# A fused transformer layer in fp16 pairs: the order of VectorE's and TensorE's work in slots 1 to 3, the first loads, and the norm scales

## What is computed

```python
ln_out = layernorm(hidden_states, ln1_s, ln1_b)
qkv = ln_out @ w_qkv + b_qkv
q, k, v = jnp.split(qkv, 3, axis=-1)
ctx = merge_heads(attention(split_heads(q), split_heads(k), split_heads(v), ltor_mask))
x = hidden_states + ctx @ w_ao + b_ao
ln_out = layernorm(x, ln2_s, ln2_b)
q = ln_out @ w_q + b_q
k, v = jnp.split(encoder_states @ w_kv + b_kv, 2, axis=-1)
ctx = merge_heads(attention(split_heads(q), split_heads(k), split_heads(v), cross_mask))
x = x + ctx @ w_co + b_co
ln_out = layernorm(x, ln3_s, ln3_b)
return x + gelu(ln_out @ w1 + b1) @ w2 + b2

def attention(q, k, v, mask):
    scores = jnp.einsum('bhqd,bhkd->bhqk', q, k) / jnp.sqrt(jnp.float32(HD))
    scores = scores * mask - 10000.0 * (1.0 - mask)
    return jnp.einsum('bhqk,bhkd->bhqd', jax.nn.softmax(scores, axis=-1), v)
```

## Time and profile before

| | |
|---|---|
| median of 3 runs | 1778.62 us (1777.15 to 1781.05) |
| the profiled execution | 1779.09 us |
| its span, first to last instruction | 1777.3 us |
| mean granted TensorE clock, as a share of full speed | 0.995 |
| busy in the span: TensorE, its weight loads | 1689.2, 1032.7 us |
| VectorE, ScalarE, GpSimd | 1033.2, 1036.9, 658.8 us |

### The profile page before, as it was taken

The page is one execution under the profiler, slowest core; times in us unless marked ns, Lnnn a source line. Parts: engine busy times, 40 slices in busy tenths (PEclk is TensorE's granted clock), DMA queues, the critical chain, the costliest instruction groups (busy, mean ns, idle before and its releaser), DMA issues. The chain is left out here.

```text
span 1777.3 us, 40192 instructions
## 1 busy us (share of the span) xinstructions
PE 1689.2 (95%) x13342; PEld 1032.7 (58%) x13342; DVE 1033.2 (58%) x3584; ACT 1036.9 (58%) x3138; POOL 658.8 (37%) x812
## 2 busy tenths in 40 slices
PE   3899999999999999999999997999999999999999
PEld 2567676766766766767667663444444444444444
DVE  6877777777776677777777764623233332324221
ACT  3677777778877777777788865532323232323332
POOL 0456556565654554655555642202020201010110
PEclk9999999999999999999999999999999999999999
DMA  5332223222231232332222312310101020202010
GB/s 157 98 103 92 89 86 100 86 64 88 92 102 52 82 111 92 112 100 97 91 94 99 116 40 94 96 60 13 59 12 65 6 66 5 71 0 71 0 48 24
DMA packets 83236, 130.31 MB, mean 73 GB/s; under 512 B 14144, under 2 KB 22336, under 8 KB 83136
## 3 DMA queue, kind: packets, MB, share of 16 engines
q1 hardware_dynamic: 83136, 129.04, 22.6%
HBM read 103.83 MB, written 25.17 MB: 73 GB/s over the span
## 5 line engine op out<-in xcount | busy, mean ns | idle before, releaser
L1253 POOL TENSOR_TENSOR a_p_s<-a_p_s,a_rcp 128x512 f32<-128x512 f32 x256 | 266.6, 1041 | 444.5 <-DVE a_rcp L889 444.4
L758 ACT ACTIVATE a_p_s<-a_t_s,a_mx 128x128 f32<-128x128 f32 x1024 | 398.7, 396 | 10.0 <-DVE a_mx L880 10.0
L1437 PE MATMUL m_ps_y<-w,m_g_r 128*128 128x512 f16 x1536 | 353.2, 379 | 0.0
L1423 PE MATMUL m_ps_h<-mlp_xT,w 128*128 128x512 f16 x1536 | 349.8, 379 | 2.0 <-PEq L407 1.7
L1522 DVE SCALAR_TENSOR_TENSOR m_g_r<-m_g_t,up_by,m_g_r 128x512 f16<-128x512 f32 x128 | 103.3, 807 | 407.0 <-ACT m_g_r L1495 406.6
L1423 PEld LDWEIGHTS m_ps_h<-mlp_xT,w 128*128 128x128 f16 x1536 | 150.0, 98 | 182.3 <-issue 2.2
L1437 PEld LDWEIGHTS m_ps_y<-w,m_g_r 128*128 128x128 f16 x1536 | 150.2, 98 | 176.6 <-DVE m_g_r L1522 0.2
L880 DVE CUSTOM_DVE_ANT_0 a_t_s<-a_ps_s,a_m_add 128x128 f32<-128x128 f32 x1024 | 231.3, 282 | 6.2 <-DVE a_ps_s L870 6.1
L1478 ACT ACTIVATE m_g_t<-m_ps_h,bias_cols,back 128x512 f32<-128x512 f32 x128 | 99.4, 776 | 222.6 <-PE m_ps_h L1423 222.6
L870 DVE TENSOR_TENSOR a_ps_s<-a_ps_s,a_m_mul 128x512 f32<-128x512 f32 x256 | 176.2, 688 | 52.3 <-PE a_ps_s L542 51.9
L749 ACT COPY a_pT<-a_ps_t 128x512 f32<-128x512 f32 x256 | 149.0, 582 | 93.9 <-PE a_ps_t L551 93.8
(11 more groups left out here) (118 smaller groups left out, 2264.5 us busy)
## 6 DMA issues: line engine op xcount, KB each, us to landing
w_stage<-in_w SPq DMA_DIRECT2D x64, 256.0 KB, 3.3
a_x_t<-in_x SPq DMA_DIRECT2D x32, 256.0 KB, 2.6
a_res_t<-in_x SPq DMA_DIRECT2D x32, 256.0 KB, 3.1
x_after_self<-a_y_t SPq DMA_DIRECT2D x32, 256.0 KB, 2.0
w_stage<-in_ctx SPq DMA_DIRECT2D x32, 256.0 KB, 3.1
a_x_t<-x_after_self SPq DMA_DIRECT2D x32, 256.0 KB, 2.7
a_enc_t<-in_ctx SPq DMA_DIRECT2D x32, 256.0 KB, 3.5
a_res_t<-x_after_self SPq DMA_DIRECT2D x32, 256.0 KB, 2.9
```

The source lines that it names most:

```text
L758: last = nc.scalar.activation(p_s[:, n % 2, j], t_s[:, n % 2, j], ACT.Exp, scale=-1.0, bias=mx[:, n % 2, j:j + 1], accum_out=sums[:, n % 2 ...
L1253: nc.gpsimd.tensor_tensor(p_s[:, n % 2], p_s[:, n % 2], rcp[:, n % 2].unsqueeze(2).to_broadcast([P, HQ, P]), ALU.mult).then_inc(s["normal" ...
L1423: last = nc.tensor.matmul(ps_h[j % 2][:], w1[hw][:, j // KC, kc, (j % KC) * P:(j % KC + 1) * P], xT[:, hx, kc], start=(k == 0), stop=(k == ...
L1437: last = nc.tensor.matmul(ps_y[b][:], g_r[:, j % 2, hg, b * P:(b + 1) * P], w2[hw][:, j // KC, j % KC], start=(j == 0 and x == 0), stop=(j ...
```

## The change

It does five things.

- In the self stage the second flip moves from the middle of slot 3 to the end of slot 2, on all three engines that take part.
- In slot 1 VectorE inverts the sums and adds the output row ahead of the scaling of block 1, which now stands directly ahead of the mask; the mask waits for the scaling.
- In slots 1 and 5 a semaphore step of VectorE carries the wait for the scaling.
- At the start the norm rows are loaded behind the keys' weights, and VectorE looks at the keys' weights ahead of `scale_norm(SELF)`.
- `scale_norm` of the cross stage and of the MLP stays in slot 3 of groups 14 and 30; the rest of `input_scales` goes to slot 5.

```diff
--- before.py
+++ after.py
@@ flips @@
                 if not crosses(g + 1):
-                    return [("x", g + 1, n - 2)] if not last and n in (2, 3) else []
+                    return [("x", g + 1, int(last))] if n == 2 else []
@@ block.sync @@
                     for b in range(GB):
                         load_x(0, b)
-                    load_norm(sp, SELF)
                     for c in range(KC):
                         load_raw(sp, WK, c)
+                    load_norm(sp, SELF)
                     load_params(sp, SELF)
@@ block.vector, slot @@
                         if n % KC == 0 and (cur if n >= 2 else prev):
                             invert_sums(*lag(g, n, 2))
+                        if n == 1 and prev:
+                            invert_sums(*lag(g, n, 2))
+                            output_row(g - 1, 0)
                         if cur:
                             scale_scores(g, n)
-                        if n == 1 and prev:
-                            if cur:
-                                dve.wait_ge(s["scaled"], at(slot_no(g, n)))
-                            invert_sums(*lag(g, n, 2))
-                        if n in (1, 4) and prev:
-                            output_row(g - 1, n // 4)
-
-                        if n % KC == 0 and cur and known(g, 1):
+                        if n == 4 and prev:
+                            output_row(g - 1, 1)
+
+                        if n % KC < 2 and cur and known(g, 1):
                             dve.wait_ge(s["scaled"], at(slot_no(g, n)))
                             dve.sem_inc(s["mask_begun"], 1)
-                        if n % KC and (cur if n >= 2 else prev and n != 1):
-                            if cur:
+                        if n % KC and (cur if n >= 2 else False):
+                            if cur and (n % KC > 1 or not known(g, 1)):
                                 dve.wait_ge(s["scaled"], at(slot_no(g, n)))
                             invert_sums(*lag(g, n, 2))
@@ input_scales @@
-                        scale_norm(st)
                         if st == CROSS:
@@ split_weights @@
                         if (g, n) in ((NG - 2, 3), (gN - 2, 3)):
+                            scale_norm(CROSS if g < NG else UP)
+                        if (g, n) in ((NG - 2, 5), (gN - 2, 5)):
                             input_scales(CROSS if g < NG else UP)
@@ block.vector, start @@
                         moments(0, b)
+                    look_self((WK,), 0)
                     scale_norm(SELF)
                     for b in range(GB):
                         centre(0, b)
                     for b in range(GB):
                         norm(0, b)
-                    look_self((WK,), 0)
```

## The result

The changed kernel takes 1789.06 us (median of 4 runs, 1788.48 to 1790.42) against 1777.88 for the kernel before in the same comparison: a ratio of 1.0055, 95% interval [1.004, 1.0069]. It is slower by 7 to 12 us. Its profiled execution took 1789.3 with a span of 1787.5, so 10.2 more than the span before.

The account below looks back on a forecast made before the run. TensorE, busy 95% of the span, was taken to bound the kernel by its program order plus gaps. Terms 1.2 + 2.9 + 1.6 + 6.8 - 1.5 - 2.9 = +8.1 gave 1786.7, 8 in 10 from 1779.5 to 1793.0.

Parts of the forecast that it names:

- Middle self groups: Slot 3's transposes wait for the flip's chain: groups 2 to 9 +0.56 each, 1 and 10 to 13 +0.46, sum +6.8.
- Group 0: Second transposes later, behind VectorE's subtraction and two statistics, +2.9; half clock after the stall +1.6, between 0 and 2.9.
- Group 14: Scales burst in slot 3: adds 0, as TensorE waits there for an output row behind VectorE's burst.
- Slots 1 and 5: VectorE's new order there: 0, as TensorE does not wait for the row and earlier normalising only widens a slack.
- Start: Norm rows land behind the weights, 9.8 to 11.9, taken as 10.5, delaying the norm scales: +1.2, ends 0 to +2.6.
- Scales: Group 30: small steps moved to slot 5 shorten TensorE's wait for the output row, -1.5; its half clock goes, -2.9.
- Rival A: Self stage: chain from flip to transposes under 3.4, so TensorE keeps its order; faster, 1768.6; chance 0.11.
- B: Norm rows behind all weights (+2.6), group 0's longer half clock (+2.9), group 30 keeps half clock: +13.7, 1792.3; chance 0.13.
- C: Self groups: late transposes swallowed by later waits of the same group; no change, +1.3, 1779.9; chance 0.13.

Follow-up runs that it names:

- the kernel with the sums first: The changed kernel with block (g,1)'s inverted sums ahead of the second subtraction, slot 3's scaling and mask still behind it: 1779.93, ratio 1.0004.

## Why the prediction was right

The forecast was 1786.7, +8.1; measured were +11.2 between the medians, +10.2 between the profiled spans, +9.8 by the ratio. Step by step:

- **Middle self groups: right.** Flip, cast, subtraction, scaling, sums, GpSimd, transposes came in the order named, 3.96 long where 3.98 was taken from the cross stage's links. Forecast +0.56, measured +0.58 at the second transposes, and nothing later took it back. The period gained 0.05 more: the scores start 0.59 behind transposes that had to wait, 0.53 behind those that had not (group 5). With groups 10 and 13, where the slots cost something, groups 1 to 13 gave +8.0 for +6.8.
- **Group 0: mechanism right, clock too small.** From first to second transposes 3.50 became 6.44, the +2.9 forecast. The half-clock stretch was forecast at +1.6, by the shorter of two examples. It was 6.8 us long with 6.30 of work in it, and the period's 5.87 less the 2.94 leave it the +2.9 of the upper bound. The stall had no TensorE work at all for 3.4 us, where the examples had 0.15 and 0.32. The change's second trace took 35.24 there, so the size differs by a microsecond between executions.
- **Group 14: wrong, +0.67 for 0.** The second transposes came 1.31 later, the keys behind them 1.37; the wait for the output row shrank by 1.01, from 2.88 to 1.87, so it swallowed most of that and not all: at the queries behind the row the two timelines are 0.36 apart. Transposes later in the group added the rest.
- **Slots 1 and 5: the sum near zero, the reason wrong.** "The normalising earlier by 0.2 only widens a slack" holds in groups 1 to 9. In group 16's slot 1 there was no slack but a wait of 1.26.
- **Start: size near by luck, reason wrong.** +0.85 for +1.2. The step that failed is the rows' landing at 9.8 to 11.9; they were there by 9.4. The look's 2.29, put between the weights' landing at 8.10 and the reduction, set the reduction's start. The 9.3 that the term was counted from was late for the old start as well, which began its reduction between 7.92 and 9.32 over seven traces. The Trainium skill, "DMA: Bandwidth & Descriptors", section "Queues, rings and completion order", has each DMA engine take descriptors in ring order. The weights did come before the rows here. But the upper end that I had set beside it, 11.9, was the landing of the old order's last piece, and that did not carry over. And in the kernel before, a weight piece issued at 2.59, behind both rows, landed at 8.4, ahead of the second row at 9.3: the order of issue was not that of landing.
- **Scales: sum right, half of it luck.** -4.24 for -4.4. In the six traces with the old scales, or kernels that keep them, group 30 took 37.20, 37.17, 37.10, 35.78, 34.32 and 34.31; in the eight with the new ones 32.76 to 32.96. So -1.4 to -1.5 is sure, and the wait fell to 1.67 where 1.7 was forecast. The half clock adds 1.7 on average (the mean of the six, 35.98, less 34.31), not the 2.9 that one trace had shown.
- **Not foreseen:** -0.7 in group 15 and -0.7 in groups 16 to 29, both from the slots (the kernel with the slots alone has them), and +0.98 - 0.49 in the tail and the MLP, both within what these stretches differ by between traces.

That the sum came within 2.1 us of the spans' +10.2 is in part luck: groups 0 to 14 were 3.2 over their terms, and the slots' -1.4 took some of that back.

Rival A was wrong: the chain is 3.96, not 3.4, so TensorE did not keep its order. But the gain of up to 0.4 a group that A promised is there in another kernel, once the subtraction leaves the chain: 0.33. B's long stretch came in group 0, but neither its late rows nor group 30's half clock. C fell with the second transposes' delay, which stays to the end of groups 0 to 13 and of which group 14 swallowed a part.

## What to carry to other kernels

When a step is moved forward on several engines at once, look at each engine's queue by itself: the producer may gain from its new place while a consumer, in order, waits in front of work that others need. Here the flip on TensorE with its cast on ScalarE gained 0.33 us a group, and the subtraction on VectorE cost 0.96; only the first two should move. And price a clock's stretch, or the landing of a load, over several traces, since one execution shows a value that the next doesn't.

## What was not expected of the hardware

The half-clock stretches are not a property of the kernel alone. Group 30's stall of 3.25 us, with the same instructions, had no half clock at its end or behind it in the second trace of the kernel before (34.31), 3.4 us in the kernel with slots 1 and 5 alone (35.78) and 6.8 us in the first trace (37.20); the runs of the kernel before spread from 1776.4 to 1783.3. Group 0's longer stall (in the kernel with the sums first, two waits of 1.25 and 2.52) had 6.8 us at half clock beginning at its end in each of its four traces.

The six first loads behind the two sequences, two norm rows and four weight pieces of 256 KB each, were all there sooner with the rows issued last: at 9.2 to 9.4 in seven traces, against 10.8 to 12.0 in the seven with the rows issued first. No run here shows why.
